# Order of TensorE's work in the first pass of a gated cross-attention and mixture-of-experts kernel: up products ahead of the first scores, second half of the queries behind the last mix

## The reference

```python
def attention(query, key, value, pad_mask, subsq_mask, Wq, bq, Wk, bk, Wv, bv):
    q, k, v = (heads of query @ Wq.T + bq, key @ Wk.T + bk, value @ Wv.T + bv)
    att = einsum('bhsd,bhtd->bhst', q, k) / sqrt(32), masked with pad_mask and subsq_mask
    return softmax(att) @ v, heads put side by side

def ffn(x):
    shared_out = (silu(x @ shared_gate) * (x @ shared_up)) @ shared_down
    topk_probs, topk_idx = top_k(softmax(x @ router), 2)
    routed = sum over the 2 chosen experts of prob * (silu(x @ gate_e) * (x @ up_e)) @ down_e
    return routed + shared_out

x = x + tanh(g_xattn[0]) * attention(layernorm(x), ctx, ctx, ...)
x = x + tanh(g_ffn[0]) * ffn(layernorm(x))
```

## Time and profile before

| | us |
|---|---|
| median of 3 runs | 1122.03 |
| profiled execution | 1132.72 |
| its span, first to last instruction | 1130.9 |
| TensorE busy in the span | 1030.5 |
| VectorE, ScalarE, GpSimd busy | 758.8, 503.0, 440.6 |
| one odd iteration of the loop | 15.68 |
| one even iteration of the loop | 16.90 |

### The profile page before, as it was taken

The page is one execution under the profiler, slowest core; times in us unless marked ns, Lnnn a source line. Parts: engine busy times, 40 slices in busy tenths (PEclk is TensorE's granted clock), DMA queues, the critical chain, the costliest instruction groups (busy, mean ns, idle before and its releaser), DMA issues.

```text
span 1130.9 us, 31209 instructions
## 1 busy us (share of the span) xinstructions
PE 1030.5 (91%) x10160; PEld 790.1 (70%) x10161; DVE 758.8 (67%) x2792; ACT 503.0 (44%) x1010; POOL 440.6 (39%) x606
## 2 busy tenths in 40 slices
PE   5787989998999999999995579999999999998997
PEld 4576888987888889888884335555555555577785
DVE  4548677895677787877764566666666666636556
ACT  2344554653566556665551144444444444311111
POOL 4323345554366555556632232222222222035543
PEclk9766798997999999999997779999999999999999
DMA  8511395543564323444227233333333335159887
GB/s 308 233 45 44 132 232 98 106 88 43 93 98 103 84 40 93 104 104 104 86 56 225 29 89 117 113 111 121 120 112 111 112 121 155 58 141 322 296 299 263
DMA packets 76754, 147.30 MB, mean 130 GB/s; under 512 B 20912, under 2 KB 23088, under 8 KB 73872
## 3 DMA queue, kind: packets, MB, share of 16 engines
q1 hardware_dynamic: 46800, 68.11, 25.8%
q0 software_dynamic: 12896, 35.58, 10.7%
q10 hardware_dynamic: 16992, 42.74, 9.8%
HBM read 94.04 MB, written 52.35 MB: 129 GB/s over the span
## 4 chain that ended last, share of the span: by engine, by line
PE 73%; DVE 9%; issue 6%; DMA 4%; ACT 3%; POOL 2%; another core or an unknown queue 1%; SPq 1%; DVEq 0%; POOLq 0%; ACTq 0%
PE bank L1165 11%; PE bank L1173 8%; PE bank L1174 8%; PE bank L1175 8%; PE bank L1269 8%; PE bank L1245 5%; PE bank L1219 4%; PE bank L1220 4%; PE bank L1221 4%; DVE arena L854 2%; PE bank L1284 2%; PE bank L1285 2%; PE bank L1286 2%; PE bank L1229 2%; DMA normed_rows<-arena 2%
## 5 line engine op out<-in xcount | busy, mean ns | idle before, releaser
L1165 PE MATMUL bank<-ident,arena 128*128 128x128 f32 (+1 forms) x1336 | 186.3, 276 | 24.2 <-ACT arena L637 15.1
L1219 PE MATMUL bank<-arena,weights 128*128 128x128 f16 x1024 | 181.7, 223 | 6.2 <-DMA arena<-normed_transposed 4.6
L1220 PE MATMUL bank<-arena,weights 128*128 128x128 f16 x1024 | 181.4, 223 | 0.0
L1221 PE MATMUL bank<-arena,weights 128*128 128x128 f16 x1024 | 181.4, 223 | 0.0
L1165 PEld LDWEIGHTS bank<-ident,arena 128*128 128x128 f32 (+1 forms) x1336 | 148.1, 145 | 46.8 <-issue 25.3
L509 POOL TENSOR_TENSOR arena<-arena 128x512 f32<-128x512 f32 x96 | 108.7, 1133 | 161.9 <-DVE arena L854 154.6
L561 POOL DMA_INDIRECT arena<-normed_rows,arena x71 | 70.9, 999 | 253.6 <-PE bank L1165 235.2
L1269 PE MATMUL bank<-arena 128*128 128x33 f32 x1024 | 140.8, 284 | 14.3 <-DVE arena L868 7.1
L1269 PEld LDWEIGHTS bank<-arena 128*128 128x128 f32 x1024 | 135.8, 205 | 19.0 <-ACT arena L604 8.6
L854 DVE CUSTOM_DVE_ANT_0 arena<-bank,arena 128x128 f32<-128x128 f32 x512 | 117.1, 286 | 41.7 <-PE bank L1245 41.1
L604 ACT ACTIVATE arena<-bank 128x512 f32<-128x512 f32 x128 | 76.4, 597 | 128.0 <-PE bank L1165 121.7
(11 more groups left out here) (192 smaller groups left out, 2270.8 us busy)
## 6 DMA issues: line engine op xcount, KB each, us to landing
expert_rows<-arena ACTq DMA_DIRECT2D x71, 256.0 KB, 2.1
arena<-in_x SPq DMA_DIRECT2D x64, 256.0 KB, 5.1
x_rows<-arena SPq DMA_DIRECT2D x48, 256.0 KB, 5.2
arena<-x_rows SPq DMA_DIRECT2D x48, 256.0 KB, 3.3
weights<-in_w_gu ACTq DMA_DIRECT2D x8, 1024.0 KB, 8.8
normed_rows<-arena SPq DMA_DIRECT2D x32, 256.0 KB, 5.4
out<-weights ACTq DMA_DIRECT2D x32, 256.0 KB, 4.5
weights<-in_w_down ACTq DMA_DIRECT2D x4, 1024.0 KB, 8.1
```

The costliest lines, as they stand in the source:

```text
L1165: last = t.transpose(dst[:, c * P:(c + 1) * P], src[:, c * P:(c + 1) * P], (ident16 if src.dtype == F16 else ident)[:, :])
L1219: t.matmul(at, shared(c, part, 0, dc), x_hi_c, start=(c == 0), stop=False)
L1220: t.matmul(at, shared(c, part, 0, dc), x_lo_c, start=False, stop=False)
L1221: last = t.matmul(at, shared(c, part, 1, dc), x_hi_c, start=False, stop=(c == EC - 1))
```

## The change

Two blocks of TensorE's program in the first pass change places with their neighbours. The up products of the shared expert are issued ahead of the first scores of an iteration, and the second half of the query projection is issued behind the last mix of values. Nothing is added or removed, and the other engines' programs are the same instruction for instruction.

```diff
--- before.py
+++ after.py
@@ -1317,9 +1317,9 @@
                             last.then_inc(fd_done, 1)
 
                 turn_probs(0)
-                scores(0)
                 shared_up(0)
                 shared_up(1)
+                scores(0)
                 mix_values(0)
                 turn_probs(1)
                 n, j, u = tile(J, v, LQ)
@@ -1341,8 +1341,8 @@
                 mix_values(2)
                 turn_probs(3)
                 queries((0, 1))
+                mix_values(3)
                 queries((2, 3))
-                mix_values(3)
                 n6, j6, u6 = tile(J, v, LX2)
                 if live(n6, NT):
                     pe.wait_ge(x2t_ready, n6 + 1)
```

## The result

| | before | changed |
|---|---|---|
| median of 7 runs each | 1123.11 (1116.44 to 1125.9) | 1132.34 (1129.76 to 1140.69) |
| ratio, 95% interval | | 1.0109 (1.0066 to 1.0151) |
| profiled execution, span | 1132.72, 1130.9 | 1138.62, 1136.3 |

The changed kernel is slower by 9.2 us by the medians, where 6.5 were forecast; its time lies in the range. The ratio is not the quotient of the two medians, which is 1.0082; the means of the seven executions are 12.2 us apart, and that is 1.09%. The ratios of the experiments, too, differ a little from the quotients of their medians. They leave out executions more than 1.5% above the fastest of their kernel.

A forecast was written before the change was run, and what follows sets the result against it. TensorE, busy for 91% of the span, was taken to bound the kernel. The sum 5.6 + 0.9 = +6.5 us, applied to the median of 1122.03, gave 1128.5 us, range 1118 to 1140.

The forecast's parts named there:

- three of the four rivals: Delay absorbed by ScalarE, 1123 us, chance 0.14; two clock falls, about 1137, 0.25; nothing shows, 1122, 0.05.
- Main term: Loop's odd iterations: queries end 0.87 us later, delaying L604, so TensorE waits 0.70 us before the first mix; 5.6 us.
- The slack of 0.17 us: Odd loop iterations before the change: how much later L604 could end without making TensorE's first mix wait.
- Up products' move: Up products ahead of first scores: VectorE's maxima start 1.35 us later in odd iterations, priced at nothing.
- the case that the cover is gone: VectorE's 1.09 us idle before odd iterations' maxima no longer covers their delay: 0.3 us each, 2 us in all.
- Even iterations: Loop's even iterations: L604's slack suffices, the 1.10 us router-exponential wait gives no credit; still 16.9 us.
- The scores covered by the up products: Scores start later behind the up products, so L666, 0.87 us later, still ends before them: no wait.
- Head: Iterations 4 to 15: iteration 7 already waits for L604, so +0.9 us; bounds -0.5 to +1.8.
- Iteration 10: TensorE's 3.05 us gap at the scores: up products must wait for L965, so no gain; as long as before.
- Rival 1, the clock: Odd iterations' 0.70 us idle makes TensorE's clock fall; two falls of 4.3 us give about 1137 us; chance 0.25.
- a granted clock under 1.00 in odd iterations: Sign in the changed profile that the forecast is wrong and the clock rival, chance 0.25, holds.

The follow-up runs named there:

- experiment 3: Changed kernel with ScalarE's conversion L718 issued behind the first norm's scaling in odd iterations, instead of ahead of L604: 1125.1 us, ratio to before 0.9994.
- Experiment 1: Kernel before with only the up products moved ahead of the first scores, queries left together: 1122.06 us, ratio to before 0.9986.
- experiment 9: Kernel before with up products ahead of the first scores and VectorE's L1044 issued early, within the odd iteration: 1117.43 us for 1126.4, ratio 0.9931.
- experiment 6: Kernel before with only VectorE's L1044 issued earlier, inside the odd iteration behind the maxima, on the second chip: 1161.98 us for 1170.48, ratio 0.9941.
- experiment 11: Kernel before with only VectorE's L1044 issued early in the odd iteration, on the third chip: 1114.73 us for 1126.4, ratio 0.9904.
- experiment 2: Kernel before with only the second half of the queries moved behind the last mix: 1134.76 us, ratio to before 1.0109.
- experiment 8: Changed kernel unedited, measured again on the second chip against the kernel before: 1172.35 us for 1170.48, ratio 1.002.
- experiment 10: Changed kernel with VectorE's L1044 issued early in the odd iteration, on the third chip: 1122.93 us for 1126.4, ratio to before 0.9968.
- experiment 12: Changed kernel unedited, measured again on the third chip against the kernel before: 1130.46 us for 1126.4, ratio 1.0066.
- experiment 5: Changed kernel with twelve up products computed a second time between first scores and first mix of the loop's odd iterations: 1128.61 us, ratio to before 1.0013.
- experiment 7: Changed kernel with ScalarE's L718 issued behind the first norm and VectorE's L1044 issued early, on the second chip: 1174.22 us, ratio to before 1.0024.

## Why the prediction was right, point by point

The forecast's mechanism is the one measured: the wait of 0.72 us, at the place and in the iterations named. That the time lies in the range says less, since the range from 1118 to 1140 also holds the times of three of the four rivals (1123, 1137 and 1122 us). The term that was mis-sized is the clock, which the sum put at nothing. And the first ratio, 1.0109, is a case (slower by over 1%) that was given a chance of 0.27; the two later ones are within 1%, which had 0.68.

- **Main term, 8 x 0.70 us: right.** The wait is 0.72 us in all eight odd iterations, put down to L604, and experiment 3 removes it by moving L718 alone. The slack of 0.17 us came from the earlier trace rows, and 0.87 - 0.17 is what appeared. Undersized was what goes with it: an odd iteration is 0.81 us longer (15.68 to 16.49), since TensorE is also busy 0.09 us more around the wait. That makes 8 x 0.81 = 6.5 us where 5.6 were priced; that it equals the whole forecast is chance.
- **Up products' move, nothing: right for this kernel.** Experiment 1 gives 0.9986. The cover was named: VectorE idle ahead of its maxima; that idle time is 3.72 us now. The second was not: nothing as long as L1044 stands behind these maxima in the odd iteration. Put it there, as experiment 9 does, and the move costs 0.9 us in each odd iteration, where the forecast had 0.3 for the case that the cover is gone.
- **Even iterations: right.** 16.84 to 16.90 us, and the wait for L637 at 1.13 to 1.18: nothing of the odd iteration's delay is given back there. Experiments 6 and 11 confirm that the wait hangs on L1044's place, since it goes when L1044 is moved.
- **The scores covered by the up products: right.** No wait of the scores for L666 in the loop; experiment 2 shows that they would wait 0.8 us in each iteration without them. What that is worth was not said: little in the loop, 0.8 us an iteration in the head.
- **Head, +0.9 us.** Iteration 7 took 20.25 us for 19.40, as forecast. Iteration 8 took 15.12 for 13.77, with 0.57 us at L604 and 0.68 more than before at a wait put down to issue. The two make 2.2 us, over the term's upper bound of 1.8. It can't be seen in the total: iteration 16 starts anywhere between 258 and 284 us in the executions profiled.
- **Iteration 10: right in the wait, wrong as a sign to look for.** L965 released the up products, as said. But the iteration took 17.70 us and not 23.12. Among the executions profiled it takes 15.5 to 26.6 us with the up products first and 15.7 to 23.1 without. The 3.05 us in the earlier trace rows belonged to that execution, not to the kernel; one execution was not enough to read it from.
- **Rival 1, the clock: it happened, beside the forecast.** The forecast named a granted clock under 1.00 in odd iterations as a sign of being wrong, and this sign came. Of the 32 odd loop iterations in the four executions in which the wait stood unfilled (31 of the 32 have it), twelve took some 18.1 us at a mean clock of 0.91: four in the first, then two, three and three (experiments 8, 10 and 12). One costs 18.13 - 16.49 = 1.6 us, a little under the 1.85 that the earlier trace rows gave and far from 4.3. That is 3.3 to 6.6 us an execution. Part of it is offset: the even iterations of three of those executions show none. In the fourth (experiment 8) another fall starts at the end of iteration 17 and leaves 17 at 0.96 and 18 at 0.95. The even iterations of the other orders do show some, one at 0.91 in the execution of before and two in that of experiment 1. I had priced the rival as all or nothing; it should have been a term of the sum, of about three falls less the one or two of before.
- **Size.** The longer odd iterations alone make 6.5 us, and +9.2, +1.9 and +4.1 us were measured by the medians in the three comparisons, by the means +12.2, +2.1 and +6.7. The first interval (1.0066 to 1.0151) and the second (0.9984 to 1.0056) do not meet. Whether the chip or the share of disturbed iterations makes that difference was not tried and stays open.

## What to carry to other kernels

When work is moved later on the engine that bounds, follow the engine that empties its result: the price is the delay less the slack at the next thing that stands behind that evacuation, here a conversion and a copy in ScalarE's queue. A block moved for nothing is free only against the kernel as it stands; once the covering wait is repaired it has a price, so repair the larger wait first (here VectorE's L1044, 0.6 to 1.0%) and then choose the order. And a gap in one profiled execution is evidence for the kernel only where it repeats in its iterations or in a second execution.

## What the runs showed of the hardware

- **A GpSimd operation stands still beside some VectorE operations.** L538 takes 0.27 us as a rule (the median of 32 in the trace of before) and 1.76 us when it starts inside L1044; in the changed kernel it ends at 413.82 + 1.76 = 415.58, L1044 at 415.45. L519 takes 0.45 us (the median of 32 before), and 2.52 us when it starts inside the same VectorE operation (L786 in experiment 11), ending 0.30 us behind it. The Trainium skill ("SBUF — State Buffer", section "SBUF: two separate sides") says that a VectorE operation with two inputs in SBUF and a GpSimd operation that reads SBUF exclude each other for the whole instruction; these ends agree. The first of the two stands at the start of the even iteration's wait, the second on the way to the waits of experiments 7 and 9; how much of them it makes was not measured by itself.
- **The same idle time went with falls of TensorE's clock in one place and with none in another.** With 0.7 us of it between small products (scores, mix, transposes; 0.46 in one) twelve iterations of 31 fell. With twelve up products in its place (experiment 5) none of eight did, and with 0.76 us of it straight behind 24 gate products (experiment 9) none either. Eight are few: at a rate of twelve in 31, none in eight would come by chance one time in fifty; and experiment 5 closes the gap and adds heavier products at once, so it does not tell which of the two keeps the clock. In all twelve the low clock starts 4.6 to 5.4 us into the iteration, where the first mix ends (3.78 + 1.08 = 4.86); of the changed kernel's iteration 27:

```profile
468.00:470.00 2.00, 2.00 (x17) 1.94 (x17) 1.46 (x9) 0.80 (x3) 1.96 (x3) 0.72 0.16 59
470.00:472.00 2.00, 2.00 (x21) 2.00 (x20) 0.69 (x1) 1.59 (x3) 1.34 (x2) 0.50 1.18 231
```

  That is 0.50, or 1.2 GHz; 15.77 and 17.44 us of busy time say what it costs. Which iterations fall differs from execution to execution (17, 23, 27, 31; 25, 29; 17, 19, 21; 21, 25, 31), and what picks them is open.
- **Chips differ more than the change does.** The same kernel before took 1124.25, 1170.48 and 1126.4 us as a median on three chips. Most of the second chip's excess lies behind the changed part: from the end of the loop to the end the four executions profiled there took 613 to 629 us, the others 583 to 590.
